# A recommendation tower whose tiles go through their stages in quarters, with a float32 projection

## The chip, the cores and the metric

The kernel runs on one core of a Trainium2 chip. The metric is the time of one execution on the device in microseconds, the median of several runs. TensorE (PE) does the matrix products, VectorE (DVE) and ScalarE (ACT) the elementwise work, GpSimd (POOL) issues the table gathers, and SyncE (SP) issues the other transfers.

## What is computed

For each of 2048 samples, 26 rows of 64 values are looked up in 26 tables, projected to 128 values, normalised, mixed over the features to 32 rows and normalised again. These 32 rows and the projected dense features `x` give 33 vectors; their pairwise products feed a linear layer with a normalisation, and then three dense layers. Constant rows and columns are left out here:

```python
x = layer_norm(dense_t @ Wd.T, gd, bd)                       # 2048 x 128
y = layer_norm(einsum('bnd,ed->bne', sparse_t, Ws), gs, bs)  # 2048 x 26 x 128
y = einsum('bne,pn->bep', y, Wsi)
y = layer_norm(y, gsi, bsi)                                  # over the 32
T = concatenate([x[:, None, :], swapaxes(y, 1, 2)], axis=1)  # 2048 x 33 x 128
Z = einsum('bnd,bmd->bnm', T, T)
out = layer_norm(Z[:, TRIL_I, TRIL_J] @ Wl.T, gl, bl)        # first 384 of 512 kept
h = relu(concatenate([z, dense], 1) @ W_top1 + b1)
y = relu(h @ W_top2 + b2) @ W_top3
```

## The kernel before

The 2048 samples are 16 tiles of 128. A tile is two blocks of 64 samples. Each block has 1664 looked-up rows, which fill 13 chunks of 128 partitions; a chunk holds 64 values of block 0 beside 64 values of block 1. So a tile is 26 gathers of 128 rows each. The chunks form four groups of 4, 4, 4 and 1.

The norm over the 128 projected values is not taken from the projection itself. With `gram = Ws Ws^T / 128` the variance of a projected row is a quadratic form of the looked-up row. So TensorE turns each chunk (`turn`, L646), ScalarE copies it out (`keep_turned`, L941), TensorE multiplies it by `gram` (`gram_product`, L656), and VectorE multiplies the product by the rows (`square_form`, L436), sums (`row_mean_square`, L444), takes the reciprocal of ScalarE's root (`row_root` L949, `row_reciprocal` L451) and scales the rows (`scale_rows`, L458). The mean square, its root and the reciprocal are one instruction each for the whole tile.

Then `mix` (L716) mixes the features of 16 samples of each block into one PSUM bank; a tile has four such banks, j = 0 to 3. `keep_high` (L912, ScalarE) rounds the bank to fp32r and `keep_low` (L388, VectorE) writes the remainder beside it, so that 64 rows of high and 64 rows of low parts fill 128 rows. `project` (L729, L730) multiplies them by the high and the low part of the projection, two fp32r products of 512 columns for each block. `keep_y` (L400) adds a bias, `square` (L896), `y_mean_square` (L410), `y_root` (L903) and `y_scale` (L417, L424) normalise, and `interact` (L681) makes the pairwise products, 32 small products for each bank. `keep_z` copies a bank out (L889 on ScalarE for banks 0 and 2, L379 on VectorE for 1 and 3). When all four are out, SyncE writes them to DRAM (`zx`, L539) and reads them back in another order (`zd`, seven transfers, L545). `linear` (L694) has five steps; `linear_root` (L966), `scale_z` (L977), `turn_z` (L701) and `keep_turned_z` (L983) normalise and turn its result. `first_layer` (L745), `relu_1` (L919), `second_layer` (L756), `relu_2` (L928), `third_layer` (L763) and `keep_out` (L934) end the tile.

Each engine runs its own written order of these steps, `tile_work`. In the body of tile t stand the rows of tile t, the `interact` and `linear` of tile t-1, the dense layers of tile t-2, and the turns and the first two Gram products of tile t+1. A step may only start when the step before it in its engine's order has been issued, and when the semaphores it waits for have been reached. The bodies are written out for tiles 0 to 3 and 14 to 17; tiles 4 to 13 are a hardware loop with two tiles in its body (`over_tiles`).

POOL runs on its own. For tile t it waits until the rows of tile t-2 are scaled (`rows_scaled`, L562), since `rows` has two buffers, and then, 13 times, adds a base to two columns of indices (L570) and issues two gathers (L574). Each group of chunks has a semaphore of its own, `gathered`, and `turn` waits for one group.

## Time and profile before

| what | value |
|---|---|
| time, median of 3 runs | 779.56 us (778.5 to 780.78) |
| the profiled execution's own time | 779.52 us |
| its span, first to last instruction | 777.7 us |
| granted TensorE clock, mean | 0.871 |
| busy: PE, DVE, POOL, ACT | 582.8, 487.4, 455.2, 294.0 us |
| instructions | 18327 |

The page gives busy time by engine, the same in 40 slices of the span, the chain of work that ended last and the costliest groups of instructions. A granted clock of 1.00 is TensorE's 2.4 GHz, 0.50 is 1.2 GHz; means between them mix the two. A group's mean is over all its instructions at either clock. "Idle before" is how long the engine sat idle just before these instructions, and `<-` names what ended the wait; `issue` means that the profile shows nothing it waited for. A float32 product stands in the trace as two MATMUL records.

### The profile page before, as it was taken

Reading aid. Unit: us, or ns where it says so; the run is one execution under the profiler, and the core shown is the slowest. Engines: PE = TensorE matmul, PEld = TensorE weight load, DVE = VectorE, ACT = ScalarE, POOL = GpSimd, SP = SyncE. Lnnn points to the kernel's source line nnn. Section 1 sums busy time; section 2 is a strip of 40 time slices with the busy share of each in tenths; the row PEclk is TensorE's granted clock in tenths of the full one; section 3 lists DMA queues with packets and bytes.
Section 4 is the critical chain, followed back from the end, with each engine's and each line's share of the span. In section 5 each row is a group of like instructions: output and inputs, shape, how many; then the busy total and the mean of one; then the engine's idle time right before and its main releaser. Section 6 shows DMA issues by size and latency. Waiting matters only on the chain.

```text
span 777.7 us, 18327 instructions
## 1 busy us (share of the span) xinstructions
PE 582.8 (75%) x6783; PEld 476.5 (61%) x6783; DVE 487.4 (63%) x773; ACT 294.0 (38%) x711; POOL 455.2 (59%) x628
## 2 busy tenths in 40 slices
PE   4447556869786987778778888678788887879767
PEld 3334344867675775657667676566667675758555
DVE  4628556559583958467574867458485867768810
ACT  1305533235353534243353334235353434344512
POOL 5666666666666666666666666666666666660000
PEclk9669787779899899998798899879899899999989
DMA  8200011020200202020210202121110202020110
GB/s 305 104 20 21 21 50 38 22 67 21 68 20 22 68 20 67 22 67 22 64 24 22 66 20 67 24 63 25 51 37 22 67 22 67 22 66 6 47 48 1
DMA packets 27200, 36.49 MB, mean 47 GB/s; under 512 B 8917, under 2 KB 17775, under 8 KB 26607
## 3 DMA queue, kind: packets, MB, share of 16 engines
q1 hardware_dynamic: 13808, 21.65, 7.9%
q0 software_dynamic: 13312, 13.66, 7.8%
q8 instruction: 64, 1.05, 0.5%
q14 instruction: 16, 0.13, 0.1%
HBM read 26.09 MB, written 9.18 MB: 45 GB/s over the span
## 4 chain that ended last, share of the span: by engine, by line
POOL 47%; issue 42%; PE 6%; POOLq 1%; DMA 1%; DVE 1%; ACT 1%; SPq 0%; DVEq 0%; ACTq 0%
POOL rows L574 41%; POOL ids L570 6%; PE bank_d L745 2%; PE bank_z L694 1%; PE bank_z L681 1%; POOLq L572 1%; PE bank_z L756 0%; POOLq L573 0%; PE bank_d L716 0%; DMA zx<-zs 0%; DVE y_var L410 0%; DMA rows<-in_table,ids 0%; PE bank_z L763 0%; PE bank_a L716 0%; DMA row_base<-in_row_base 0%
## 5 line engine op out<-in xcount | busy, mean ns | idle before, releaser
L574 POOL DMA_INDIRECT rows<-in_table,ids x416 | 407.0, 978 | 237.7 <-issue 198.8
L681 PE MATMUL bank_z<-r_vec 128*32 128x35 f32 x4096 | 77.6, 204 | 48.1 <-issue 47.3
L681 PEld LDWEIGHTS bank_z<-r_vec 128*32 128x32 f32 x4096 | 58.3, 112 | 71.7 <-issue 67.3
L896 ACT ACTIVATE y_sq<-y 128x512 f32<-128x512 f32 x128 | 75.3, 626 | 66.5 <-DVE y L400 55.8
L379 DVE COPY zs<-bank_z 128x280 f32<-128x280 f32 x32 | 14.4, 450 | 126.2 <-PE bank_z L681 65.9
L694 PE MATMUL bank_z<-wl,zd 128*128 128x512 f32 x160 | 83.2, 639 | 8.4 <-DMA zd<-zx 8.4
L424 DVE TENSOR_TENSOR r_vec<-y,y_r 128x512 f32<-128x512 f32 x128 | 83.3, 692 | 2.2
L912 ACT CAST mixed<-bank_d 64x512 fp32r<-64x512 f32 x64 | 37.1, 580 | 124.4 <-PE bank_d L716 66.0
L729 PE MATMUL bank_b<-mixed,proj_hi 128*128 128x512 f32 x64 | 36.5, 570 | 61.8 <-DVE mixed L388 59.9
L410 DVE TENSOR_REDUCE y_var<-y_sq 128x32 f32<-128x1024 f32 x64 | 77.4, 1210 | 0.7 <-ACT y_sq L896 0.7
L912 ACT CAST mixed<-bank_a 64x512 fp32r<-64x512 f32 x64 | 37.1, 579 | 75.5 <-PE bank_a L716 55.0
L745 PE MATMUL bank_d<-z_t,w 128*128 128x128 f32 x384 | 64.7, 312 | 0.0
L646 PE MATMUL bank_z<-ident,rows 128*128 128x128 f32 x208 | 38.6, 306 | 33.5 <-DMA rows<-in_table,ids 31.2
L646 PEld LDWEIGHTS bank_z<-ident,rows 128*128 128x128 f32 x208 | 30.2, 161 | 51.0 <-DMA rows<-in_table,ids 36.4
L388 DVE TENSOR_TENSOR mixed<-bank_a,mixed 64x512 fp32r<-64x512 f32 x64 | 44.1, 689 | 26.7 <-ACT mixed L912 22.7
L729 PEld LDWEIGHTS bank_b<-mixed,proj_hi 128*128 128x128 f32 x64 | 13.8, 215 | 75.2 <-DVE mixed L388 69.0
L716 PE MATMUL bank_d<-wsi_b,scaled 128*128 128x192 f32 (+3 forms) x256 | 58.3, 388 | 0.0
L716 PEld LDWEIGHTS bank_d<-wsi_b,scaled 128*128 128x128 f32 x256 | 55.5, 258 | 3.8
L694 PEld LDWEIGHTS bank_z<-wl,zd 128*128 128x128 f32 x160 | 44.7, 303 | 21.4 <-issue 12.5
L745 PEld LDWEIGHTS bank_d<-z_t,w 128*128 128x128 f32 x384 | 56.5, 221 | 1.5 <-ACT z_t L983 0.5
L436 DVE TENSOR_TENSOR scaled<-bank_b,rows 128x512 f32<-128x512 f32 x32 | 22.0, 687 | 54.5 <-PE bank_b L656 45.5
L570 POOL TENSOR_TENSOR ids<-ids_all,row_base 128x2 int32<-128x2 int32 x208 | 48.0, 231 | 7.3 <-DMA row_base<-in_row_base 3.1
(114 smaller groups left out, 1012.7 us busy)
## 6 DMA issues: line engine op xcount, KB each, us to landing
zx<-zs SPq DMA_DIRECT2D x16, 560.0 KB
rows<-in_table,ids POOLq DMA_INDIRECT x416
dense_t<-in_dense_t SPq DMA_DIRECT2D x1, 2048.0 KB
wl<-in_wl SPq DMA_DIRECT2D x1, 1280.0 KB
w<-in_w SPq DMA_DIRECT2D x1, 1280.0 KB
zd<-zx SPq DMA_DIRECT2D x16, 80.0 KB
wsi_b<-in_wsi_b SPq DMA_DIRECT2D x1, 1248.0 KB
zd<-zx SPq DMA_DIRECT2D x16, 70.0 KB
```

The source lines that it names most:

```text
L410: v.tensor_reduce(y_var[:, j, :], y_sq[:, j % 2, :, :].rearrange("e a (s p) -> e (a s) p", p=PROJ), AX_X, ALU.add).then_inc(y_var_done, 1)
L424: ins = v.tensor_tensor(r_vec[:, quad:quad + SPB // QUAD, :, Y0:PAD], y[:, Y_PART[j], blk, :].rearrange("e (g s p) -> e g s p", g=SPB // Q ...
L570: nc.gpsimd.tensor_tensor(ids[par][:, n:n + 2], ids_all[:, bass.ds(t * (2 * CHUNKS) + n, 2)], row_base[:, n:n + 2], ALU.add).then_inc(ids_ ...
L574: nc.gpsimd.indirect_dma_start(rows[par][:, c, D * blk:D * (blk + 1)], None, io["table"], bass.IndirectOffsetOnAxis(ap=ids[par][:, n:n + 1 ...
L646: mm = pe.transpose(bank_t[g % 2][:, n * P:(n + 1) * P], rows[par][:, c, :], ident[:])
L681: mm = pe.matmul(bank_z[PROJ * s:PROJ * (s + 1), j, n * ITEMS:(n + 1) * ITEMS], own[:, Y0:PAD], own, start=True, stop=True)
L694: mm = pe.matmul(bank_l, zd[:, :, s], wl[:, s, :], start=(s == 0), stop=(s == STEPS - 1))
L716: mm = pe.matmul(bank_m[j % 2][:, o:o + k * PROJ], scaled[:, c, :], wsi_b[:, w0:w0 + k, :], start=(n == 0), stop=(n == len(wins) - 1), ski ...
L729: pe.matmul(bank_g[blk][:], proj_hi[:], mixed[:, j % 2, blk, :], start=True, stop=False)
L745: mm = pe.matmul(bank_d[:, k * TILE:(k + 1) * TILE], w1[:, c, k * P:(k + 1) * P], z_t[:, c, :] if c < 3 else dense[c - 3], start=(c == 0), ...
L896: nc.scalar.activation(y_sq[:, j % 2, blk, :], y[:, Y_PART[j], blk, :], ACT.Square)\
L912: nc.scalar.copy(mixed[own, j % 2, blk, :], bank_m[j % 2][own, :]).then_inc(mix_hi, 1)
```

## The change

The groups of chunks become 4, 3, 3 and 3, one for each bank of `mix`. All steps up to `interact` are now written for a quarter k = 4 t + q. Each of the three compute engines runs a plain unrolled list of 72 stages; the hardware loop is gone from them, and POOL keeps its own. In stage w stand the rows, `mix` and `project` of quarter w, and the norm of y, `interact` and `keep_z` of quarter w-1. The parts that belong to a whole tile stand at fixed quarters.

The root, the mean square and the reciprocal of the rows are taken for one quarter. The high/low split is gone: `keep_low` and the two halves of `keep_high` give way to one copy of the bank, `keep_mixed`, on ScalarE, and `project` is one float32 product over 64 rows for each block, block 0 on rows 0 to 63 and block 1 on rows 64 to 127. All four `keep_z` of a tile are on ScalarE. `mix` has one PSUM bank where it had two, turned chunks and Gram products share one bank, and `interact` has one bank where it had four.

The core of the diff:

```diff
-GROUPS = [range(c, min(c + 4, CHUNKS)) for c in range(0, CHUNKS, 4)]
+GROUPS = [range(0, 4), range(4, 7), range(7, 10), range(10, 13)]
...
+BANKS = MIX_BANKS
+QUARTERS = BANKS * TILES
+STAGES = QUARTERS + 2 * BANKS
...
-        mixed = sb("mixed", [P, 2, 2, BANK], F32R)
-        y = sb("y", [P, 3, 2, BANK])
+        mixed = sb("mixed", [P, 2, BANK])
+        y = sb("y", [P, 2, 2, BANK])
...
-        bank_g = [bank_b, bank_c]
-        bank_m = [bank_a, bank_d]
+        bank_y = [bank_b, bank_c]
+        bank_m = bank_a
+        bank_x = [bank_a, bank_d]
+        bank_t = bank_g = bank_z[:, 0, :]
+        bank_i = bank_z[:, 1, :]
+        bank_w = bank_z[:, 2, :]
         bank_l = bank_z[:, 3, :]
```

VectorE's list:

```diff
+            for w in range(STAGES):
+                tile, q = divmod(w, BANKS)
+                new, old = w < QUARTERS, 1 <= w <= QUARTERS
+                if old:
+                    y_mean_square(w - 1)
+                if new:
+                    square_form(w)
+                    row_mean_square(w)
+                if old:
+                    y_reciprocal(w - 1)
+                    y_scale(w - 1, 0)
+                if new:
+                    row_reciprocal(w)
+                    scale_rows(w)
+                if old:
+                    y_scale(w - 1, 1)
+                if w == 1:
                     last_step_weights()
...
+                if q == 3 and 1 <= tile <= TILES:
+                    linear_reciprocal(tile - 1)
+                if new:
+                    keep_y(w, 0)
+                    keep_y(w, 1)
```

TensorE's new `project` and list:

```diff
+            def project(k):
+                for blk in range(2):
+                    pe.wait_ge(mix_kept, k + 1)
+                    if k:
+                        pe.wait_ge(y_kept, 2 * (k - 1) + blk + 1)
+                    half = slice(D * blk, D * (blk + 1))
+                    pe.matmul(bank_y[blk][:], gs_row[half, :], mixed[half, k % 2, :], start=True, stop=True)\
+                        .then_inc(y_done, 1)
...
+            for w in range(STAGES):
+                tile, q = divmod(w, BANKS)
+                new, old = w < QUARTERS, 1 <= w <= QUARTERS
+                top = 2 <= tile <= TILES + 1
+                if new:
+                    turn(w)
+                if top and q == 0:
+                    turn_z(tile - 2)
+                if top and q == 2:
+                    second_layer(tile - 2)
+                if top and q == 3:
+                    third_layer(tile - 2)
+                if new:
+                    gram_product(w)
+                if w < 4:
+                    add_up_x(w)
+                if w == 1:
+                    fold()
+                if w == 4:
                     fold_bl()
...
+                if top and q == 0:
+                    first_layer(tile - 2, range(0, 2))
+                if top and q == 1:
+                    first_layer(tile - 2, range(2, 4))
+                if 1 <= tile <= TILES and q == 2:
+                    linear(tile - 1, range(0, 2))
+                if 1 <= tile <= TILES and q == 3:
+                    linear(tile - 1, range(2, STEPS))
+                if new:
+                    mix(w)
+                if old:
+                    interact(w - 1)
+                if new:
+                    project(w)
```

ScalarE's list:

```diff
+            def keep_mixed(k):
+                act.wait_ge(mix_done, k + 1)
+                if k >= 2:
+                    act.wait_ge(y_done, 2 * (k - 1))
+                nc.scalar.copy(mixed[:, k % 2, :], bank_m[:]).then_inc(mix_kept, 1)
...
+            for w in range(STAGES):
+                tile, q = divmod(w, BANKS)
+                new, old = w < QUARTERS, 1 <= w <= QUARTERS
+                top = 2 <= tile <= TILES + 1
+                if old:
+                    square(w - 1, 0)
+                    square(w - 1, 1)
+                if new:
+                    keep_turned(w)
+                if top and q == 0:
+                    keep_turned_z(tile - 2)
+                if old:
+                    y_root(w - 1)
+                if new:
+                    row_root(w)
...
+                if 1 <= tile <= TILES and q == 1:
+                    place_sum_x(tile - 1)
+                if 1 <= tile <= TILES and q == 3:
+                    linear_root(tile - 1)
+                if top and q == 2:
+                    relu_2(tile - 2)
+                if top and q == 3:
+                    keep_out(tile - 2)
+                if new:
+                    keep_mixed(w)
+                if 1 <= tile <= TILES and q == 3:
+                    scale_z(tile - 1)
+                if old:
+                    keep_z(w - 1)
+                if new and q == 0:
+                    place_x(tile)
+                if top and q == 1:
+                    relu_1(tile - 2)
```

## Rows read from the trace of the kernel before

**Rows 1.** The page: the chain that ended last, share of the span by engine.

```profile
POOL 47%; issue 42%; PE 6%; POOLq 1%; DMA 1%; DVE 1%; ACT 1%; SPq 0%; DVEq 0%; ACTq 0%
```

**Rows 2.** Groups by line: busy us, mean ns of one, idle us before them and its releaser.

```profile
L424 DVE TENSOR_TENSOR r_vec<-y,y_r 128x512 f32<-128x512 f32 x128 | 83.3, 692 | 2.2
...
L681 PE MATMUL bank_z<-r_vec 128*32 128x35 f32 x4096 | 77.6, 204 | 48.1 <-issue 47.3
L410 DVE TENSOR_REDUCE y_var<-y_sq 128x32 f32<-128x1024 f32 x64 | 77.4, 1210 | 0.7 <-ACT y_sq L896 0.7
L896 ACT ACTIVATE y_sq<-y 128x512 f32<-128x512 f32 x128 | 75.3, 626 | 66.5 <-DVE y L400 55.8 <-issue 10.7
```

**Rows 3.** Timeline of POOL, 161 to 165: start us, us, engine, line, what, idle before.

```profile
161.21 0.96 POOL L574 DMA_INDIRECT rows<-in_table,ids  x1 [0.81 <-issue]
...
164.44 0.96 POOL L574 DMA_INDIRECT rows<-in_table,ids  x1 [0.81 <-issue]
```

**Rows 4.** Line L574 alone: min/median/max ns, start of the first and of the last.

```profile
L574 POOL DMA_INDIRECT rows<-in_table,ids x416: 938/957/1471, 4.7 to 699.5; - x139
```

**Rows 5.** Timeline, 701 to 778: the last turn and the last tile's end.

```profile
701.88 0.33 PE L646 MATMUL bank_z<-ident,rows 128*128 128x128 f32 x1 [0.79 <-DMA rows<-in_table,ids]
...
749.05 0.45 DVE L379 COPY zs<-bank_z 128x280 f32<-128x280 f32 x1 [2.73 <-PE bank_z L681]
...
756.57 6.70 PE L694 MATMUL bank_z<-wl,zd 128*128 128x512 f32 x10 [7.56 <-DMA zd<-zx]
...
763.31 0.60 ACT L966 ACTIVATE l_sq<-bank_z 128x512 f32<-128x512 f32 x1 [14.11 <-PE bank_z L694]
...
775.95 0.25 SPq L549 DMA_DIRECT2D out<-out_row  x1
```

**Rows 6.** Timeline, 703 to 719: work at full TensorE clock.

```profile
703.84 1.06 PE L656 MATMUL bank_b<-gram,rows_t 128*128 128x128 f32 x8
...
710.96 0.32 DVE L451 RECIPROCAL row_r<-row_std 128x26 f32<-128x26 f32 x1 [0.39 <-ACT row_std L949]
...
711.31 0.69 DVE L458 TENSOR_TENSOR scaled<-rows,row_r 128x512 f32<-128x512 f32 x1
...
716.07 1.14 ACT L919 ACTIVATE h<-bank_d,b 128x128 f32<-128x128 f32 x4 [1.08 <-PE bank_d L745]
...
716.89 0.77 PE L681 MATMUL bank_z<-r_vec 128*32 128x35 f32 x64
...
717.59 1.33 PE L716 MATMUL bank_d<-wsi_b,scaled 128*128 128x128 f32 x8
```

**Rows 7.** Timeline, 437 to 446: ScalarE and TensorE at full clock in the loop.

```profile
437.12 0.59 ACT L941 COPY rows_t<-bank_z 128x512 f32<-128x512 f32 x1
...
437.92 1.13 PE L694 MATMUL bank_z<-wl,zd 128*128 128x512 f32 x2
...
444.02 1.95 PE L756 MATMUL bank_z<-h,w 128*128 128x128 f32 x16
```

**Rows 8.** Timeline of TensorE, 159 to 161, one `interact` in an unrolled body.

```profile
159.29 0.98 PE L681 MATMUL bank_z<-r_vec 128*32 128x35 f32 x44
160.72 0.40 PE L681 MATMUL bank_z<-r_vec 128*32 128x35 f32 x20 [0.46 <-issue]
```

**Rows 9.** Timeline, 32 to 60: first turns, first Gram product at half clock.

```profile
32.63 1.97 PE L646 MATMUL bank_z<-ident,rows 128*128 128x128 f32 x8 [2.24 <-DVE x_t L332]
...
50.02 1.91 PE L656 MATMUL bank_b<-gram,rows_t 128*128 128x128 f32 x8
...
55.01 2.74 PE L616 MATMUL bank_z<-wl,fold_w 128*65 128x512 f32 x6
```

**Rows 10.** Timeline of TensorE, 474 to 477, a `mix` at half clock.

```profile
474.84 2.44 PE L716 MATMUL bank_d<-wsi_b,scaled 128*128 128x96 f32 x8
```

**Rows 11.** Stretches of 3 us: busy us of PE, PEld, DVE, ACT, POOL; PEclk, DMA.

```profile
431.00:434.00 3.00, 2.52 (x7) 2.09 (x8) 2.22 (x4) 0.00 (x0) 1.87 (x4) 0.50 0.52 173
...
443.00:446.00 3.00, 3.00 (x22) 2.53 (x21) 2.97 (x7) 2.25 (x6) 2.40 (x3) 1.00 0.07 15
```

More of the change, by code:

```diff
@@ L86, in block_rows, with group_of @@
     return PLACES[k][0], PROJ - PLACES[k][1]
+def group_of(c):
+    return next(g for g, chunks in enumerate(GROUPS) if c in chunks)
 WINDOWS, WIN_COLS = chunk_windows()
@@ new lines, in linear @@
+            def linear(t, steps):
+                if steps[0] == 0:
+                    pe.wait_ge(z_moved, Z_MOVES * (t + 1))
+                    pe.wait_ge(sumx_placed, t + 1)
+                    if t:
+                        pe.wait_ge(z_kept, t)
+                    else:
+                        pe.wait_ge(wl_centred, 1)
+                for s in steps:
+                    mm = pe.matmul(bank_l, zd[:, :, s], wl[:, s, :], start=(s == 0), stop=(s == STEPS - 1))
+                if steps[-1] == STEPS - 1:
+                    mm.then_inc(l_done, 1)
@@ L776, in tile_work @@
-                if top:
-                    first_layer(0)
-                if inter:
-                    interact(0)
-                    interact(1)
-                if top:
-                    first_layer(1)
-                if load and not inter:
-                    fold(range(0, 1))
-                    fold(range(1, 3))
-                if load:
-                    mix(0)
-                if top:
-                    first_layer(2)
-                if load and not inter:
-                    add_up_x(0)
@@ L792, in tile_work @@
-                if top:
-                    first_layer(3)
-                if load:
-                    project(0)
-                if inter:
-                    interact(2)
-                if load:
-                    mix(1)
-                if load and not inter:
-                    fold(range(3, STEPS))
-                if load:
-                    mix(2)
-                if inter:
-                    interact(3)
-                if load:
-                    project(1)
-                    mix(3)
@@ L809, in tile_work @@
-                if more:
-                    turn(t + 1, 1 - par, 0)
-                if load and not inter:
-                    add_up_x(1)
-                if load:
-                    project(2)
-                if more:
-                    turn(t + 1, 1 - par, 1)
-                if load and not inter:
-                    add_up_x(2)
-                if inter:
-                    linear(range(0, 1))
-                if load:
-                    project(3)
-                if inter:
-                    linear(range(1, 3))
@@ L825, in tile_work @@
-                if more:
-                    turn(t + 1, 1 - par, 2)
-                if load and not inter:
-                    add_up_x(3)
-                if inter:
-                    linear(range(3, STEPS))
-                if more:
-                    turn(t + 1, 1 - par, 3)
-                if inter and not top:
-                    fold_bl()
-                if top:
-                    second_layer()
-                if more:
-                    gram_product(t + 1, 0)
-                    gram_product(t + 1, 1)
```

653 lines of the change are left out of this document (234 added, 419 removed).

## The prediction, made before the changed kernel was run

> **What bounds the kernel now.** I read the chain of waits first. It is POOL and its issue time for nearly nine tenths of the span [rows 1]: the gathers follow one another without a wait for the other engines, and the rest of the chain is the last tile. A pair of gathers with its index instruction takes 3.23 us [rows 3], 13 pairs 42.1 us. The last of the 416 starts at 699.5, the first at 4.7 [rows 4], which is 43.5 us a tile; the difference is gathers that stretch beyond their median of 0.957. The last data are turned at 701.9 [rows 5]. From there to 777.7 the whole last tile still has to pass: 75.8 us. So the kernel is 702 us of gathers and 76 us of tail. PE, DVE and ACT keep up, since each fills its waits with work of neighbouring tiles.
>
> The change leaves POOL's instructions as they are. It can gain only in the tail, and it can lose if the new lists of the other engines need more than 43.5 us for four stages.
>
> **The stage as a loop.** In the new lists one path runs round through all three engines. DVE's last step of stage w-1 is `keep_y`; ACT's squares wait for it, ACT's `keep_turned` stands behind the squares, the Gram product behind that, and so on to the next `keep_y`. I add it up from the end of a `keep_y`, at full clock and for 4 chunks. A hand-over costs 0.03 us (711.28 to 711.31 in [rows 6]); I take 0.04.
> - second square 0.63 [rows 2], copy of the turned chunks started 0.07 before its end, 0.59 [rows 7]: 1.2. Gram product 1.06 [rows 6]: 2.3.
> - `square_form`: the 0.69 of a 512-column DVE operation [rows 2, 6]: 3.0. Mean square of 512 elements: half of 1.21 for 1024 [rows 2] and some start-up, 0.69: 3.7. The root on ACT runs beside DVE's `y_reciprocal` (0.34, from 0.32 for 26 columns [rows 6]) and first `y_scale` 0.69 [rows 2]: 4.7. Reciprocal of 8 columns 0.2 (estimate, under that 0.32), `scale_rows` 0.69 [rows 6]: 5.6.
> - `mix` 1.33 [rows 6]: 6.9. `keep_mixed` 0.59 (as the copy in [rows 7]) lies beside `interact` of the quarter before, 0.77 [rows 6]: 7.7.
> - `project`: one float32 product of 512 columns is two records, 1.13 together [rows 7]: 8.8. The two `keep_y`, spaced 0.6, end at 10.1 if block 1 comes 0.43 after block 0, at 10.3 if 0.86.
> So 10.2 us. With 3 chunks five of these steps lose a quarter, 0.75 in all: 9.45. Four stages are 38.6.
>
> What is removed (two `keep_low`, 0.69 each by the nearest DVE row, per bank, the second half copy, two fp32r records per block) is thus partly returned as a longer path, since nothing now separates the steps.
>
> Of the whole-tile work, `first_layer` and `linear` lie in TensorE's 3.3 us between Gram product and `mix` and cost nothing at full clock; `turn_z`, `linear_root`, `scale_z` and `keep_z` lie beside DVE. Two don't: `second_layer` (1.95 [rows 7]) stands before the Gram product, which could start at 1.2, and costs 0.8; `relu_1` (1.14 [rows 6]) is last in ACT's list, before the next squares, and costs 0.6. That gives 40.0 us a tile, 3.5 less than POOL. SyncE's transfers need 7.1 us from the last `keep_z` to `linear` (749.5 to 756.6 [rows 5]); they have one and a half stages. DVE holds about 6.3 us of each stage, ACT 4.8: neither binds by its sum. POOL waits only if scaling lags the landing by more than about 36 us (43.5 less some 7).
>
> **Two costs the trace gives only in part.** `interact` is 128 very short instructions. They start late 48.1 us in all, 0.75 us a bank [rows 2]; in one body a bank takes 1.83 us instead of 0.77 [rows 8]. Now `project` waits directly behind it. Bounds 0 and 3.0 us a tile; I take 1.5, because TensorE waits before every `mix` and its supply can refill.
> The Trainium skill (Runtime: NRT & Kernel Launch, Instruction fetch mechanics) says a taken branch breaks sequential prefetch, so unrolling would help. Rows 8 are from a body written out before the loop and show the gap all the same; the rule would give at most these 3.0 us, the rows nothing, and I count no gain.
> The clock is the other. Its mean is 0.871, so it is at half speed a quarter of the time. It fell where TensorE had waited or run thin, and rose under dense work [rows 11]. At half clock the path grows by 0.85 in the Gram product [rows 9], 1.1 in `mix` [rows 10], 0.8 in `project` and about 0.75 in `interact`: 3.5 a stage, 14 a tile. The new path has no TensorE wait over 1.5 us where the old one had waits over 3 on the split, so I take a tenth of the time: 1.4 a tile; bounds 0 and 3.6.
>
> **The beginning.** Stage 0 starts at 32.6 as before [rows 9] and takes 13 us at half clock. Stages 1 to 7 are 9.45 each, one 10.2: 67. Without dense layers TensorE is thin, so I take half clock half the time, 12, plus 3 for short supply; `fold` (six records 2.74 [rows 9], ten 4.5) and the once-only weight steps behind it 5. Stage 8 starts at 132, 27 us after its rows land at about 105. POOL's limit of 36 is not met.
> From there 56 stages, 14 tiles of 42.9: stage 63 ends at 132 + 601 = 733. The lag has shrunk to about 20 us.
>
> **The new tail.** After stage 63: squares, mean square, root, reciprocal, two scales 4.0, `interact` 0.8, `keep_z` 0.4, transfers 7.1: `linear` starts at 12.3 and takes 6.7 at mostly half clock [rows 5]: 19.0. From there to the end nothing changes: 763.3 to 777.7, 14.4 [rows 5]. Together 33.4. The span is 733 + 33.4 = 766.4; the profiled execution lies 1.8 above its span (779.52 to 777.7), and equals the median within 0.04. I predict **768 us**, 1.5% faster.
>
> **The rivals.**
> A. The forecast: the loop of waits sets the pace, under POOL's. Tile 41.6 to 43.4, time 750 to 775.
> B. POOL stays the bound. A tile under 41.4 works off the lag. Then stage 63 starts at the landing, 701.9, and ends 9.6 later, at 711.5; with 33.4 and 1.8 this is 747 us. For it: 40.0 before the two uncertain costs. Against: both have to stay small.
> C. The loop is slower than POOL. From 43.8 us a tile the gain of the tail is used up (132 + 613 + 35 = 780). At 44.5 it is 790, at 45.2 800. For it: the clock. If it stays at 0.87 as before, a tile is 45 and the time 798. A slower stage also thins TensorE, which keeps the clock down. Against: the long waits on `keep_low` are gone.
> D. The change doesn't do what it says. In A and C quarters are not taken as they land, but queue 20 us or more behind the gathers; only in B does the landing start the stage.
>
> **How the numbers follow.** A 0.42, B 0.18, C 0.33, and 0.07 for the strip between A and C, 43.4 to 43.8 us a tile, within 0.3% of before. A measurement can tell about 0.3% from no change. Faster 0.60, same 0.07, slower 0.33. The range leaves out B with shorter stretches of POOL below, and C above 45.2 us a tile: 745 to 800.
>
> **What would show it.** The chain of waits: in A and C it goes round DVE, ACT and PE, and POOL ends near 700 with its share of the chain small; in B it is still POOL. `gathered` would hardly appear as a releaser of `turn` in A. `mix` follows `scale_rows` by 0.05, the wait of `project` is on `interact` or the copy. Granted clock above 0.9 speaks for A or B, at 0.87 or under for C. The idle before `interact` tells whether 1.5 was right. From the last `keep_z` to the end should stay 28.2. The prediction is wrong if POOL itself is slowed, by waiting for `rows_scaled` or by more DVE collisions; then its last gather moves from 699.5.

## The result

The changed kernel takes **756.14 us** (median of 3 runs, 755.08 to 758.15), the kernel before 779.56. The ratio is 0.970, with a 95% interval of 0.966 to 0.974: 3.0% faster. The forecast was 768 us with a range of 745 to 800, so the direction and the range held and the size was half of what came. The profiled execution has a span of 756.3 us and a granted clock of 0.903 (before: 777.7 and 0.871). Here and below, ratios leave out executions more than 1.5% above the fastest of the same kernel, and medians don't.

The mechanism of the forecast did not come about. I had expected the loop of waits through VectorE, ScalarE and TensorE to set the pace (case A). The page of the changed kernel shows case B: the chain of waits is still GpSimd and its issue time. This is part 4 of the page, shares of the span:

```profile
POOL 49%; issue 43%; PE 4%; DMA 2%; POOLq 1%; ACT 1%; SPq 0%; DVE 0%; DVEq 0%; ACTq 0%
```

The groups of instructions by line of the changed kernel say the same, busy time, mean ns and idle time with its releasers. L602 is `turn`, L642 is `interact`, L629 is `project`:

```profile
L602 PE MATMUL bank_z<-ident,rows 128*128 128x128 f32 x208 | 40.4, 312 | 51.1 <-DMA rows<-in_table,ids 48.9 <-DVE x_t L329 2.2
L642 PE MATMUL bank_z<-r_vec 128*32 128x35 f32 x4096 | 56.1, 203 | 0.2
L629 PE MATMUL bank_b<-mixed,gs_row 64*128 64x512 f32 x128 | 74.2, 660 | 0.8 <-ACT mixed L801 0.7
```

TensorE waits 48.9 us for gathered rows, which case A excluded. `interact` starts late by 0.2 us in all, where [rows 2] have 48.1.

The starts of `mix` give the pace. These are stages 8, 28 and 60 in the timeline of TensorE (start, duration, idle before):

```profile
135.89 1.38 PE L619 MATMUL bank_a<-wsi_b,scaled 128*128 128x160 f32 x8 [1.09 <-DVE scaled L402]
...
333.49 1.38 PE L619 MATMUL bank_a<-wsi_b,scaled 128*128 128x160 f32 x8 [1.10 <-DVE scaled L402]
...
682.63 1.32 PE L619 MATMUL bank_a<-wsi_b,scaled 128*128 128x160 f32 x8
```

From stage 8 to 28 a tile takes (333.49 - 135.89) / 5 = 39.5 us: the loop runs faster than the gathers and works off its lag. From 28 to 60 it takes (682.63 - 333.49) / 8 = 43.6 us, the pace of the gathers. The mean over 13 tiles is 42.1.

The last tile, in the timeline of the changed kernel, TensorE with the two `keep_z` of ScalarE and the last gathers of GpSimd:

```profile
702.70 1.27 POOL L534 DMA_INDIRECT rows<-in_table,ids  x1 [0.81 <-POOL ids L530]
704.28 0.94 POOL L534 DMA_INDIRECT rows<-in_table,ids  x1 [0.31 <-issue]
...
707.48 0.55 PE L602 MATMUL bank_z<-ident,rows 128*128 128x128 f32 x3 [1.63 <-DMA rows<-in_table,ids]
...
709.51 4.29 PE L655 MATMUL bank_z<-wl,zd 128*128 128x512 f32 x6
713.63 1.31 PE L619 MATMUL bank_a<-wsi_b,scaled 128*128 128x96 f32 x8
...
723.27 0.77 PE L642 MATMUL bank_z<-r_vec 128*32 128x35 f32 x64
...
724.08 0.39 ACT L808 COPY zs<-bank_z 128x280 f32<-128x280 f32 x1 [3.74 <-PE bank_z L642]
...
733.23 3.60 PE L655 MATMUL bank_z<-wl,zd 128*128 128x512 f32 x4 [3.48 <-DMA zd<-zx]
...
737.28 2.95 PE L655 MATMUL bank_z<-wl,zd 128*128 128x512 f32 x6
```

Between the turn of the last rows and the end lie 756.3 - 707.5 = 48.8 us, where [rows 5] have 75.8: 27 us less. The last rows are turned 5.6 us later than in [rows 5] (707.5 against 701.9). The difference is the 21.4 us between the spans.

### The profile page after: what moved, and what is told of

The parts are those of the page before. It is cut to its first block, busy times and chain, and to the rows that moved or that the text cites. A ratio compares the mean times of both kernels' runs of the same rounds, so it can differ in the third digit from the quotient of the medians.

```text
span 756.3 us, 17826 instructions
## 1 busy us (share of the span) xinstructions
PE 574.3 (76%) x6783; PEld 431.4 (57%) x6783; DVE 407.5 (54%) x707; ACT 293.2 (39%) x727; POOL 460.0 (61%) x628
## 4 chain that ended last, share of the span: by engine, by line
POOL 49%; issue 43%; PE 4%; DMA 2%; POOLq 1%; ACT 1%; SPq 0%; DVE 0%; DVEq 0%; ACTq 0%
POOL rows L534 42%; POOL ids L530 6%; PE bank_z L655 1%; PE bank_d L675 1%; DMA zx<-zs 1%; POOLq L532 1%; POOLq L533 0%; DMA rows<-in_table,ids 0%; DMA row_base<-in_row_base 0%; PE bank_z L686 0%; SPq L505 0%; PE bank_z L693 0%; DMA zd<-zx 0%; PE bank_z L642 0%; POOLq L526 0%
## 5 line engine op out<-in xcount | busy, mean ns | idle before, releaser
L412 DVE TENSOR_TENSOR y<-bank_b,y_bias 128x512 f32<-128x512 f32 x64 | 44.3, 691 | 176.3 <-PE bank_c L629 95.2
L619 PE MATMUL bank_a<-wsi_b,scaled 128*128 128x192 f32 (+3 forms) x512 | 91.7, 325 | 39.9 <-DVE scaled L402 39.9
L619 PEld LDWEIGHTS bank_a<-wsi_b,scaled 128*128 128x128 f32 x512 | 81.1, 201 | 70.5 <-DVE scaled L402 68.7
L608 PE MATMUL bank_z<-gram,rows_t 128*128 128x128 f32 x416 | 74.0, 326 | 57.8 <-ACT rows_t L786 57.3
L608 PEld LDWEIGHTS bank_z<-gram,rows_t 128*128 128x128 f32 x416 | 61.4, 223 | 71.8 <-ACT rows_t L786 71.8
L801 ACT COPY mixed<-bank_a 128x512 f32<-128x512 f32 x64 | 37.5, 586 | 136.8 <-PE bank_a L619 136.7
L602 PEld LDWEIGHTS bank_z<-ident,rows 128*128 128x128 f32 x208 | 23.9, 152 | 102.6 <-DMA rows<-in_table,ids 74.1
L602 PE MATMUL bank_z<-ident,rows 128*128 128x128 f32 x208 | 40.4, 312 | 51.1 <-DMA rows<-in_table,ids 48.9
L629 PE MATMUL bank_b<-mixed,gs_row 64*128 64x512 f32 x128 | 74.2, 660 | 0.8 <-ACT mixed L801 0.7
L629 PE MATMUL bank_c<-mixed,gs_row 64*128 64x512 f32 x128 | 72.6, 648 | 0.0
L377 DVE TENSOR_TENSOR scaled<-bank_z,rows 128x512 f32<-128x512 f32 (+1 forms) x64 | 37.8, 591 | 60.7 <-PE bank_z L608 57.3
L642 PE MATMUL bank_z<-r_vec 128*32 128x35 f32 x4096 | 56.1, 203 | 0.2
L642 PEld LDWEIGHTS bank_z<-r_vec 128*32 128x32 f32 x4096 | 46.9, 111 | 10.0 <-issue 3.6
## 6 DMA issues: line engine op xcount, KB each, us to landing
wsi_b<-in_wsi_b SPq DMA_DIRECT2D x1, 1248.0 KB, 11.4
```

The lines of the kernel that those rows point to most:

```text
L602: mm = pe.transpose(bank_t[:, n * P:(n + 1) * P], rows[t % 2][:, c, :], ident[:])
L608: mm = pe.matmul(bank_g[:, n * P:(n + 1) * P], rows_t[:, c, :], gram[:], start=True, stop=True)
L619: mm = pe.matmul(bank_m[:, o:o + num * PROJ], scaled[:, c, :], wsi_b[:, w0:w0 + num, :], start=(n == 0), stop=(n == len(wins) - 1), skip_g ...
L629: pe.matmul(bank_y[blk][:], gs_row[half, :], mixed[half, k % 2, :], start=True, stop=True)\
L642: mm = pe.matmul(bank_i[PROJ * s:PROJ * (s + 1), n * ITEMS:(n + 1) * ITEMS], own[:, Y0:PAD], own, start=True, stop=True)
```

## The experiments

They ran on several chips, each beside the kernel before on the same chip, and the chips differ: the kernel before had medians from 780 to 801 us. So a time is compared with the kernel before that ran beside it. "Late starts" are idle time ahead of the short `interact` products for which the profile shows nothing waited for (`issue`).

### The split put back, and the projection alone

The changed kernel with the high/low split (two half copies, two `keep_low`, four fp32r products):

```diff
-nc.scalar.copy(mixed[:, k % 2, :], bank_m[:]).then_inc(mix_kept, 1)
+for blk in range(2):
+    own = slice(D * blk, D * (blk + 1))
+    nc.scalar.copy(mixed[own, k % 2, blk, :], bank_m[own, :]).then_inc(mix_hi, 1)
...
-pe.matmul(bank_y[blk][:], gs_row[half, :], mixed[half, k % 2, :], start=True, stop=True)
+pe.matmul(bank_y[blk][:], proj_hi[:], mixed[:, k % 2, blk, :], start=True, stop=False)
+pe.matmul(bank_y[blk][:], proj_lo[:], mixed[:, k % 2, blk, :], start=False, stop=True)
```

> The changed kernel with the high/low split put back, nothing else: keep_high in two half copies, two keep_low on VectorE, four fp32r products of 128 rows. Counted from the end of mix by rows of the kernel before: first half 0.6, keep_low 0.7 (1.3), the second 2.0, the products of block 1 2.6, keep_y 2.0 to 2.6 and 2.6 to 3.2. The changed kernel needs copy 0.6, interact 0.8, project 1.1, two keep_y 1.2, together 3.1 behind the wait. If this sum holds, the stage grows only by 0.1 to 0.3 us, a tile is 41 to 42 us, GpSimd stays the bound and the time is 756 to 762 us. Rival: the split was what kept the loop from fitting. Then a stage grows by 1 us or more, a tile is 44 us or more, VectorE, ScalarE and TensorE lead the chain of waits, and the time is 775 to 830 us.

Measured: 775.3 us, ratio 0.988 (0.983 to 0.993). The chain of waits was PE 43%, issue 26%, DVE 21%, a tile took 43.3 us. By time and chain that is the rival, though the tile stays under its 44 us. But a second thing differed too, which I had not put in either theory: `interact` started late by 31.5 us in all. These are the groups of this kernel (L657 is `interact`):

```profile
L657 PE MATMUL bank_z<-r_vec 128*32 128x35 f32 x4096 | 74.4, 205 | 31.5 <-issue 30.7
```

So this run could not tell the price of the split from that of the late starts. The changed kernel itself didn't run on this chip.

The kernel before with the projection alone (float32 over 64 rows, no `keep_low`, whole tiles):

> The kernel before with the projection alone changed: float32 over 64 rows, one copy of the bank, no keep_low; whole tiles as before. If the gain comes from the tail alone, and the tail from taking quarters as they land, the last gather stays near 700 us and only some waits on keep_low leave the last tile: 774 to 779 us. Rival: the lighter projection shortens the last tile by four times the 3 us that TensorE waited for the split, so that much of the gain of 23 us is the projection's: 765 to 769 us.

Measured: ratio 1.004 (0.9995 to 1.009), no gain, and both theories had a gain. The last gather started at 698.4, and TensorE turned its rows only at 709.0: `linear` waited 52.8 us in all, 51.6 of them on the transfers of `zd`. In the kernel before it waited 8.4 us on them, and `project` 59.9 on `keep_low`. So a wait on the split went and one on the transfers came. The projection alone, in whole tiles, doesn't bring the gain; what it is worth in quarters comes further down.

### Where the late starts come from

First the branch. The kernel before with the lists of TensorE, VectorE and ScalarE written out (the diff is shortened):

```diff
-with eng.Fori(2, TILES // 2 - 1) as i:
-    body(i * 2, 0, True, True, True, True)
-    body(i * 2 + 1, 1, True, True, True, True)
+for t in range(4, TILES - 2):
+    body(t, t % 2, True, True, True, True)
```

> The kernel before with the lists of TensorE, VectorE and ScalarE written out over all tiles, GpSimd's loop kept. If the late starts of the short interact products come from the taken branch of the loop, the idle time ahead of them falls from 48 us to under 10 us. If they come from what stands around interact, it stays at 40 to 50 us. Either way the time is 777 to 781 us, since GpSimd is the bound.

Measured: 788.7 us (one execution), and the idle time ahead of `interact` stayed:

```profile
L685 PE MATMUL bank_z<-r_vec 128*32 128x35 f32 x4096 | 80.8, 206 | 52.3 <-issue 51.3
```

It isn't the branch. The Trainium skill (Runtime: NRT & Kernel Launch, Instruction fetch mechanics) holds a taken branch responsible for fetch stalls; here the idle time is as long without one (52.3 us against 48.1).

Then the order of work. The changed kernel with `first_layer` and `linear` between `mix` and `interact`:

```diff
 if new:
     mix(w)
+if top and q == 0:
+    first_layer(tile - 2, range(0, 2))
...
 if old:
     interact(w - 1)
```

> The changed kernel with first_layer and linear placed between mix and interact instead of ahead of mix. If interact starts at once because TensorE waits ahead of mix and its instructions can come in meanwhile, the idle time ahead of interact grows from 0.2 us to 20 us or more, since a run of products now ends directly ahead of it. If it starts at once for another reason (one bank of 32 products at a time instead of four), the idle stays under 3 us. The products now lie on the path from mix to project: 1 to 2.4 us more for a stage, so that a tile passes 44 us and the time is 785 to 830 us.

Measured: 1031 us. The idle of `interact` came to 31.1 us as expected, but the split kernel, without this move, had 31.5 on the same chip, so it says nothing on the order. The time was 200 us beyond my bound. One stage of it, TensorE's timeline:

```profile
637.87 2.55 PE L619 MATMUL bank_a<-wsi_b,scaled 128*128 128x160 f32 x8 [3.33 <-DVE scaled L402]
640.22 1.54 PE L675 MATMUL bank_d<-z_t,w 128*128 128x128 f32 x6
641.55 1.06 PE L675 MATMUL bank_d<-dense_t,w 128*128 128x128 f32 x4
642.40 1.49 PE L675 MATMUL bank_d<-z_t,w 128*128 128x128 f32 x6
...
644.42 0.58 PE L642 MATMUL bank_z<-r_vec 128*32 128x35 f32 x42
```

The products had filled TensorE's wait ahead of `mix`. Moved, they leave a wait of 3.3 us there, and what stands right behind it runs at half clock: `mix` 2.55 for 1.33, `first_layer` 4.2 (640.2 to 644.4) for 2.4. 4.2 + 1.2 and the longer `interact` are 6 us a stage; three stages of a tile took 14.6 to 17.3 us, the fourth 11 to 14. My sum had taken the moved work at full clock.

Whether number and place of the instructions decide was tried with `project` in four products of 256 columns for two of 512, the same work:

> The changed kernel with each of the two float32 products of project split into two of 256 columns: four instructions for two, the same work. With the split put back, interact ran short of instructions in half of the stages (31 us idle and 18 us of longer spans, where the changed kernel has 0.2). If the number and place of the instructions in TensorE's list decide that, the shortage comes back here: idle ahead of interact over 5 us. If it hangs on the later start of project or on the timing of the loop, idle stays under 2 us and the time at 756 to 760 us.

Measured: 785.9 us, idle ahead of `interact` 35.0 us. By the rule written down that spoke for the place of the instructions. That reading was wrong, as the unchanged kernel on yet another chip shows:

> The changed kernel as it is, beside the kernel before on the chip on which the next three run. A kernel with the same list for TensorE up to stage 61 showed 28 us of late starts in interact on another chip, where the first trace of the changed kernel had 0.2 us. If the supply of instructions differs from chip to chip, this trace can show idle time ahead of interact of 0 to 30 us with a time of 756 to 790 us, and the kernel before is over 780 us where it is high. If it belongs to the program, idle is under 1 us and the time 755 to 758 us.

Measured: 784.0, 785.8, 797.8 and 825.1 us (median 791.8), against 799.6 for the kernel before beside it. The first two, which a ratio would count, are 2% under it. The same program as in the result, and it has the late starts; its chain of waits begins with PE 52%, issue 22%, DVE 15%:

```profile
L642 PE MATMUL bank_z<-r_vec 128*32 128x35 f32 x4096 | 73.0, 205 | 33.3 <-issue 32.7
```

A tile took (709.18 - 150.71) / 13 = 43.0 us between the same two stages. So the program doesn't decide it alone. The four products had been measured on a chip with late starts: a kernel with the same list up to stage 61 had 34.0 us there (the first attempt on the tail, below). For the chip of the split this isn't shown, since the changed kernel didn't run on it. The split once more, now beside this run:

> The changed kernel with the high/low split put back, a second time, now on the same chip as the changed kernel itself. If the split has a price of its own it is 0.4 us or more a stage longer than the changed kernel in stages without late starts (10.07 against 9.85 on average so far) and 5 to 17 us slower. Rival: the 16 us by which it was slower than the changed kernel came from the chip, and both are within 3 us here.

Measured: 788.1, 790.4, 798.4 and 800.1 us (median 794.4). The medians differ by 2.6 us, the rival's 3. But a ratio would count 788.1, 790.4 and 798.4 against 784.0 and 785.8, which speaks for a price of the split. The traces (a tile takes 44.9 us for 43.0) can't be compared, since the one is of the execution of 800.1 and the other of that of 784.0. So few executions are inconclusive.

### What the loops take without the gathers

Here the gathers after tile 1 are left out, so the later tiles compute on the rows of the first two:

```diff
-over_tiles(pool, gather)
+gather(0, 0, True, True, False, False)
+gather(1, 1, True, True, True, False)
```

> The changed kernel without the gathers after tile 1 (the later tiles compute on the rows of the first two; everything else is there). If the late starts in interact come from GpSimd's gathers, they are gone on every chip: idle under 1 us after 90 us, a tile of 39.3 us (stages of 10.22, 9.47, 9.42, 10.22), stage 8 at about 128, the end at 128 + 14 x 39.3 + 36 = 714 us, 710 to 725. If they come from the chip alone, a tile stays at 40 to 42 us and the time is 725 to 760 us.

> The same with the high/low split put back: quarters, split, no gathers after tile 1. It gives the split's own price. From undisturbed stages (9.88, 9.88, 9.87, 10.66, 40.3 us a tile) it is 1.0 us a tile: 14 to 17 us more than the one without split and gathers, 725 to 740 us. If the split only seemed dear because the chip was slower, the two are within 5 us.

> The kernel before without the gathers after tile 1. It gives the pace of the old lists: with them under 43.5 us a tile GpSimd was the bound and had room. If they need 38 to 41 us, the end is at 690 to 740 us and the new order of work is not faster as a loop, only in its tail; if 42 to 43.5, the old lists had next to no room and the time is 740 to 765 us.

Measured, on a chip where the kernel before takes 795.8: 715.5, 740.3 and 664.8 us. Stages 8 and 60 of the first, then of the second:

```profile
140.10 1.38 PE L620 MATMUL bank_a<-wsi_b,scaled 128*128 128x160 f32 x8 [1.10 <-DVE scaled L402]
...
643.80 1.38 PE L620 MATMUL bank_a<-wsi_b,scaled 128*128 128x160 f32 x8 [1.10 <-DVE scaled L402]
```

```profile
136.22 1.38 PE L635 MATMUL bank_a<-wsi_b,scaled 128*128 128x160 f32 x8 [1.10 <-DVE scaled L407]
...
669.05 1.38 PE L635 MATMUL bank_a<-wsi_b,scaled 128*128 128x160 f32 x8 [1.10 <-DVE scaled L407]
```

That is 38.7 us a tile for the changed kernel and 41.0 with the split, each over the 13 tiles between these stages. The split costs 2.2 us a tile, twice what I had expected of it; it would still leave room under 43.5, though only 0.4 under the forecast's 41.4, the tile at which the lag is just worked off. The lists of the kernel before take 35.3 us a tile (494.3 us from the first to the fifteenth `scale_z`, 14 tiles), and the whole kernel 664.8, where neither theory went under 690. So the new order is the slower loop. All that the change gains is in the tail.

And nearly all late starts are gone, on a chip that had them (35.0 us with the four products). `interact` in the changed kernel and in the kernel before, both without gathers:

```profile
L643 PE MATMUL bank_z<-r_vec 128*32 128x35 f32 x4096 | 52.9, 203 | 3.9 <-issue 3.5 <-DVE r_vec L437 0.5
```

```profile
L682 PE MATMUL bank_z<-r_vec 128*32 128x35 f32 x4096 | 49.0, 203 | 6.8 <-issue 6.8
```

The gathers cause them. In the changed kernel this shows within the one execution: the last of the 52 gathers starts at 91 us, and all 3.5 us without a releaser lie before 95. In the kernel before the 6.8 us lie behind it, so a small part of its late starts has another cause.

### Gathers closer together

The most surprising runs were meant as a simple speed-up. All index additions in one instruction ahead, GpSimd's list written out, so that gathers follow each other 0.3 us apart:

```diff
-if blk == 0:
-    nc.gpsimd.tensor_tensor(ids[par][:, n:n + 2], ids_all[:, bass.ds(t * (2 * CHUNKS) + n, 2)],
-                            row_base[:, n:n + 2], ALU.add).then_inc(ids_ready, 1)
-    pool.wait_ge(ids_ready, t * CHUNKS + c + 1)
...
-bass.IndirectOffsetOnAxis(ap=ids[par][:, n:n + 1], axis=0)
+bass.IndirectOffsetOnAxis(ap=ids_sum[:, at:at + 1], axis=0)
```

> The changed kernel with all index additions in one GpSimd instruction ahead of the gathers and GpSimd's list written out, nothing else. The gathers then follow each other faster (0.96 us and 0.3 between, about 33 us a tile), so that the three other engines set the pace and the trace shows what their loop takes by itself. If GpSimd is the bound of the changed kernel, its own loop is the 39.9 us a tile at which the trace after caught up with the gathers: stage 8 at 130, 14 tiles of 40 to 41, tail 33 to 36: 725 to 745 us. Rival (my forecast of 42.9 us a tile): 765 us or more, hardly under the changed kernel.

> The kernel before with the same faster gathers. It shows whether the loop of the kernel before had room too. If the change made the loop faster, the kernel before now falls behind its gathers: a tile of 42 to 45 us and 765 to 785 us. If the old loop had as much room as the new one (40 us a tile), it is 735 to 750 us, and the new order of work is worth only its tail.

Measured: 1242.7 us (ratio 1.56) and 1157.0. Both theories missed by 500 us. To tell whether the written-out list or the missing pauses do it, GpSimd's loop was kept and only the number of gathers for one index instruction changed. The code adds `m` columns at a time, m being 26, 4 and 1 for the 2 of the changed kernel:

```diff
-if blk == 0:
+if n % m == 0:
```

> The changed kernel with one index instruction for a tile (26 columns) in place of 13; GpSimd keeps its loop, and 26 gathers follow each other 0.3 us apart. In the kernel with all additions ahead and GpSimd's list written out, VectorE, ScalarE and TensorE stood still while gathers ran 0.3 us apart (from 440 to 460 us nothing ran on them, TensorE had one transpose every 2.4 us at 35 to 52). If gathers without the pause between pairs are what holds the others up, that comes back: 1100 to 1250 us. If it was GpSimd's list without a loop, it doesn't: 725 to 760 us.

> The changed kernel with one index instruction for four gathers in place of two, so half of the pauses of 1.1 us (index instruction and wait) are gone and a tile of gathers takes 43.5 - 6.5 x 0.5 to 0.8 = 38 to 40 us. If a pause every four gathers is enough for the other engines, they set the pace at 40 to 41 us a tile and the time is 735 to 750 us. If they are held up in proportion to the pauses taken away, the time is 780 us or more.

> The changed kernel with one index instruction and wait ahead of every gather, not of every second: a pause of 1.1 us each time. A tile of gathers takes 26 x 2.0 = 51 to 53 us, so the time is 860 to 900 us in any case. If pauses are what lets the other engines have their instructions, the late starts in interact fall under 5 us in all. If they have another cause, they stay at 20 to 50 us.

Measured: 1235.2 us for 26, 1077.6 for 4 (ratio 1.35), 915.3 for 1. The kernel with 26 gathers in a row, its timeline while GpSimd gathers without a pause:

```profile
428.23 0.30 PE L643 MATMUL bank_z<-r_vec 128*32 128x35 f32 x5 [0.45 <-issue]
...
428.99 0.28 PE L643 MATMUL bank_z<-r_vec 128*32 128x35 f32 x6 [0.46 <-issue]
...
451.77 0.69 DVE L412 TENSOR_TENSOR y<-bank_b,y_bias 128x512 f32<-128x512 f32 x1 [25.25 <-issue]
...
456.67 0.69 DVE L412 TENSOR_TENSOR y<-bank_c,y_bias 128x512 f32<-128x512 f32 x1 [4.21 <-issue]
```

and its stretches, during the gathers and after them (TensorE, its weight loads, VectorE, ScalarE, GpSimd busy; clock; DMA):

```profile
434.00:458.00 24.00, 0.37 (x1) 0.00 (x0) 1.38 (x2) 1.62 (x3) 18.09 (x20) 0.50 0.14 26
458.00:470.00 12.00, 5.83 (x34) 5.64 (x35) 4.95 (x8) 1.61 (x5) 0.95 (x1) 0.64 0.04 6
470.00:497.00 27.00, 22.05 (x301) 15.82 (x299) 16.67 (x29) 11.98 (x29) 0.00 (x0) 1.00 0.11 35
```

First `interact` gets 5 or 6 products every 0.75 us, then VectorE waits 25 us for nothing that the profile shows; in 24 us six instructions run on three engines. When the gathers stop, all goes on. The DMA engines carry 26 GB/s meanwhile, so the rows come in, and the profile shows nothing that VectorE waited for. Gathering (33 us) and computing (40 us) hardly overlap any more, and a tile takes 70.2 us, nearly their sum. What holds the engines up isn't shown. The profile counts the DMA packets that bring instructions: none from 429 to 459 us, while the gathers run, and three in the next 30 us; but engines that stand still need none, so this can be cause or consequence.

With one pause for every gather the late starts of `interact` were 19.3 us, not under 5 as expected, where related kernels had 34.0 and 35.0 on the same chip: more pauses help and don't cure. The time was 15 us over the bound. The idle ahead of `interact` alone is no measure of the hold-up: it is 119.0 us with 4 gathers in a row and 20.7 with 26, where other steps stand still instead.

### The tail

The tail was longer than case B had it, and TensorE was at half clock in it. A first attempt moved all of `linear` of tile 14 into stage 62, `first_layer` behind the last `interact`, and added seven products whose result isn't used:

> The changed kernel with its last two tiles reordered and TensorE kept busy in the last waits. linear of tile 14 goes as a whole into stage 62, and first_layer of tile 14 behind the last interact: the terms of 1.0 and 1.2 us by which stage 63 and the last keep_z came late should go, 2 us together. Seven additional products whose result isn't used (six of 512 columns, one of 256) stand in the waits of stages 66 to 68; if half clock is what makes linear 7.0 and first_layer 6.3 us, these go to about 4.5 and 4.2 and the time falls by 3 to 5 us more: 750 to 752 us where the changed kernel has 756. Rival: the waits ahead of linear (transfers) and relu set the tail and the clock doesn't come up in time: 754 to 756 us.

Measured: median 825 us, from 790 to 860, on a chip with the kernel before at 801; the time says nothing, the trace does. Without `linear` to fill it, stage 63 waited 2.9 us ahead of `mix` and ran at half clock (`mix` 2.61, `project` 1.22 a record), and four products put the last `linear` off by 4 us (it starts 12.8 us after the last `keep_z` for 8.7). From its start to the end it was then 19.8 us for 23.1. Gained 3.3, lost more. The second attempt reorders nothing and has three products ahead of the last `linear`, two behind it, one ahead of `first_layer`:

```diff
+if w == QUARTERS + 2:
+    keep_clock(3)
 if 1 <= tile <= TILES and q == 2:
     linear(tile - 1, range(0, 2))
...
+if w == QUARTERS + 3:
+    keep_clock(2)
```

It ran beside the changed kernel:

> The changed kernel as it is, a third time. If the late starts are low here as in the first trace (idle ahead of interact under 1 us), the ratio to the kernel before is 0.965 to 0.975; if they are 25 to 35 us as on the two other chips, a tile takes 42 to 43.5 us and the ratio is 0.98 to 0.99.

> The changed kernel with six additional products on TensorE in the last waits (three of 512 columns before linear of the last tile, two of 512 after it, one of 256 before first_layer), whose result isn't used; nothing is reordered. linear and first_layer of the last tile then run at full clock: from the start of linear to the end 19.6 us where the changed kernel had 23.1 and 21.5; and since three products end before the transfers land, linear isn't put off. 2 to 3.5 us less than the changed kernel beside it. Rival: the products run at half clock themselves (1.7 us each) and put linear off by 1.5 us or more, so that nothing is gained, as with four products and a reordered list (linear 4 us late, then 3.3 us faster).

Measured: the changed kernel 760.5 us, ratio 0.975 (0.973 to 0.978), `interact` idle 0.1 us; with the six products **754.9 us**, ratio 0.969 (0.967 to 0.971), the lowest of all kernels that compute everything. `linear` of the last tile, first in the changed kernel of this run, then with the products (L698):

```profile
736.32 3.79 PE L655 MATMUL bank_z<-wl,zd 128*128 128x512 f32 x4 [3.91 <-DMA zd<-zx]
740.04 1.01 PE L693 MATMUL bank_z<-h,w 128*1 128x128 f32 x4
740.99 3.56 PE L655 MATMUL bank_z<-wl,zd 128*128 128x512 f32 x6
```

```profile
729.62 2.74 PE L698 MATMUL bank_z<-x_t,ones 128*128 128x512 f32 x6
732.20 1.88 PE L655 MATMUL bank_z<-wl,zd 128*128 128x512 f32 x4
734.01 0.60 PE L693 MATMUL bank_z<-h,w 128*1 128x128 f32 x4
734.54 2.95 PE L655 MATMUL bank_z<-wl,zd 128*128 128x512 f32 x6
```

`linear` halves, 3.79 to 1.88 for four records. From its start to the end it is 752.0 - 732.2 = 19.8 us for 759.0 - 736.3 = 22.7. That is 2.9 of the 7.0 us between the two spans (the medians are 5.65 apart). The last gather starts at 704.8 for 707.0, another 2.2, and it isn't shown that the products have to do with that. And `linear` starts 7.7 us after the last `keep_z` for 9.2, which isn't the clock: the transfer of `zx` takes 2.7 us for 5.1. In the changed kernel a packet that brings instructions lies beside it, both here and in the result (4.8 us); with the six products, none does. The products did cost something: `linear` starts as the third of them ends, without idle time before it.

## Why the prediction was right and wrong

The sum for a tile is what failed: 42.9 us, where the tile between stages 8 and 28 took 39.5, and 41.4 was the border under which GpSimd stays the bound. All three of its terms were too large: the full-clock loop by 1.3, short supply by 1.1, half clock by 1.0. No one of them alone brings the sum under 41.4. So the loop of waits didn't set the pace, and the path that did, GpSimd's gathers and the tail behind them, ended earlier.

**What bounds the kernel.** Right. Without the gathers both loops run faster than GpSimd's 43.5 us, the old one at 35.3.

**The full-clock loop, 40.0 us a tile.** Its stages are right, its additions aren't. Alone it is 38.7. The stages of 10.2 and 9.45 us come out as added: in the run without gathers most tiles are 10.22, 9.45, 9.40 and 9.43. (The prediction takes 0.75 off for 3 chunks; a quarter of the five rows would be 0.93, and 0.77 was measured. Its 13 pairs of 3.23 us are 42.0, not 42.1.) What failed is the 1.4 for `second_layer` and `relu_1`; at most one stage in some tiles grows, by 0.8. Block 1 of `project` doesn't come 0.43 after block 0 but beside it. This is one stage of the changed kernel:

```profile
704.71 0.69 PE L629 MATMUL bank_b<-mixed,gs_row 64*128 64x512 f32 x1
704.75 0.67 PE L629 MATMUL bank_c<-mixed,gs_row 64*128 64x512 f32 x1
705.24 0.59 PE L629 MATMUL bank_b<-mixed,gs_row 64*128 64x512 f32 x1
705.25 0.59 PE L629 MATMUL bank_c<-mixed,gs_row 64*128 64x512 f32 x1
```

Four records of 0.6 each in 1.13 us: the two row halves work at once. The Trainium skill (TensorEngine Tiling (Array Packing), Key Properties) says so of tiles, and the trace agrees. The drain at a mode change, which the same section of the Trainium skill states, isn't seen: the sum without any drain is 38.6 to 40.0 us, and the tile takes 38.7.

**Short supply, 1.5 us a tile.** Mis-sized, and its reason failed. It was taken between bounds of 0 and 3.0. Where the result was measured it is 0.4 us a tile: by the groups above a bank of `interact` takes (56.1 + 0.2) / 64 = 0.88 us on average for 0.77. On the chip of the second run of the same kernel it is 3.6: (73.0 + 33.3) / 64 = 1.66. That is over the upper bound, which had counted the idle time of [rows 2] and not that the busy time grows too. The value between them occurred in none of the three traces of this kernel. The reason given, that TensorE's wait ahead of `mix` refills the supply, was no reason: that wait is 39.9 us in all in the one and 42.9 in the other.

**Half clock, 1.4 us a tile.** Too much. From stage 8 to 28 the granted clock is near 0.97, and 39.5 - 38.7 - 0.4 leaves 0.4 us. (The run without gathers, from which the 38.7 comes, has 0.98 itself.)

On the chip with late starts the forecast tile was met to the tenth (43.0), which is luck: 38.7 and 3.6 stand there for 40.0, 1.5 and 1.4. Case A came with it, though at 784 us and not at its 750 to 775: TensorE leads the chain there, and the gain is 2%, not 3%. The size of the late starts belongs to the gathers and the chip, which one trace can't tell.

**The start.** Right where the result was measured: stage 8 started at 130.2 (the end of `keep_y` of stage 7), forecast 132. On the chip with late starts it was 14 us later.

**The tail.** 33.4 us behind stage 63, and 9.6 for that stage: 43.0 in all. It was 48.8. Stage 63 takes 10.6, since `linear` of tile 14 runs 4.3 us at half clock just ahead of its `mix` (+1.0). The last `keep_z` comes 6.4 later, not 5.2, behind `first_layer` at half clock. The transfers take 8.7 for 7.1, `linear` 7.0 for 6.7, and the rest 16.0 for 14.4, where I had written that nothing changes. For the most part it is one cause: a tail of short steps leaves TensorE waiting, and half clock was charged to the loop but not to the tail. The run with six additional products takes 2.9 us of it back. The 1.6 of the transfers is another: `zx` lands after 4.8 us beside a packet that brings instructions, and in the kernel before its `zd` is issued after 2.95.

**GpSimd unslowed.** Named as what would make the prediction wrong, and it moved: the last gather starts at 704.3, in [rows 4] at 699.5. The gathers take 992 ns on average for 978; times 416 this is 5.8 us, about the 4.8. Runs alone differ by about half of that: in two other traces with the same gathers the last starts at 707.0 and 704.8. With 0.8 more for the landing and 5.8 from the tail it is the 11.4 us between the span of 756.3 and the 744.9 that case B gives without its 1.8. Why they stretch wasn't tried; that they do so more beside VectorE, as the 1.27 us one above, is argued only.

**Rivals.** B had 0.18 and occurred; A had 0.42 and is what the changed kernel shows on another chip, in its chain and its tile, not in its time. C occurred in the run with `first_layer` moved: a loop slower than the gathers thins TensorE, the clock falls (0.79 on average), the loop slows further, 60 us a tile. D, quarters not taken as they land, held until the lag was worked off.

**Open.** Why the changed kernel has no late starts on two chips where the kernel before, on one of them, has 48 us; and by what the gathers hold the others up. That it is the supply of instructions is read off the idle time without any releaser and the bursts of 5 products, not shown.

## What to carry to other kernels

When an engine bounds a kernel, ask what is left behind its last instruction: here the reordered lists are the slower loop (38.7 for 35.3 us a tile without gathers) and win because a quarter of a tile is left to do, not a whole one. A disputed cost with bounds of 0 and 3 us was 0.4 on one chip and 3.6 on another; give each end its own case rather than the middle. And before you take a pause out of a GpSimd list of gathers, measure what the other engines do meanwhile. A few products without a use in TensorE's last waits halve the time of those behind them (3.79 to 1.88 us), if they end before the data comes: three did nearly, four put the last `linear` off by 4 us.

## What was not expected of the hardware

- Gathers 0.3 us apart stop the other engines: six instructions in 24 us on VectorE, ScalarE and TensorE. With a pause of 1.1 us for every 2 gathers the kernel takes medians of 756 to 792 us, for every 4 it takes 1078, for every 26 it takes 1235. The Trainium skill (Runtime: NRT & Kernel Launch, Instruction fetch mechanics) says that fetching hides behind issuing. Without gathers the runs agree (3.9 us idle ahead of 4096 short products). With them there is idle time without a releaser (33 us, and 119 with 4 gathers in a row); whether it is fetching isn't shown.
- The same program has 0.2 us of late starts on one chip and 33 on another, and takes 756 or 784 us. The gain of the change is 3.0%, 2.5% and 2% on three chips.
- Two float32 products of 64 rows on different row halves and different banks run side by side for their whole length: their records start 0.01 to 0.13 us apart, at half clock too.
- The last tile's transfer of 560 KB (`zx`) lands after 2.7 us in the run with six products, and after 4.8 and 5.1 us in the two traces of the changed kernel in which a 16 KB packet of instructions runs beside it.
